# Layer kernel on one core: attention's output turned on VectorE in 32x32 blocks, the first norm's rows turned by transposing transfers, the weights' low halves made on VectorE

## What is computed

```python
mod = (_silu(c) @ wmod).reshape(8, 6, 1, 256)
sa, ca, ga, sb, cb, gb = (mod[:, i] for i in range(6))
h = layernorm(x) * (1 + ca) + sa
x = x + ga * attention(h, w_qkv, w_o)     # 16 heads of 16, causal, softmax
h = layernorm(x) * (1 + cb) + sb
x = x + gb * (shared_ffn(h) + routed_experts(h))   # 8 experts, 2 per token
```

## Time and profile before

| | us |
|---|---|
| median of the runs | 1907.32 |
| the profiled execution | 1906.43 |
| its span | 1904.7 |
| PE busy | 1759.5 (92%) |
| VectorE (DVE) busy | 1506.3 (79%) |
| ScalarE (ACT) busy | 1126.2 (59%) |
| GpSimd (POOL) busy | 955.2 (50%) |
| mean granted TensorE clock | 0.971 |

### The profile page before, as it was taken

How to read it: one execution, slowest core, us unless ns; L and a number is a source line. 1 busy time by engine, 2 the same in 40 slices (tenths; PEclk the granted TensorE clock), 3 DMA queues, 4 the chain that set the end, 5 groups by cost and what they waited for, 6 DMA issues and landing times. The chain is left out here.

```text
span 1904.7 us, 46834 instructions
## 1 busy us (share of the span) xinstructions
PE 1759.5 (92%) x17886; PEld 1014.6 (53%) x17886; DVE 1506.3 (79%) x2717; ACT 1126.2 (59%) x1486; POOL 955.2 (50%) x1015
## 2 busy tenths in 40 slices
PE   5677899999999999999999999999999999989987
PEld 2233435455554454445454545454545788778764
DVE  7886788887988787788878888988896486755777
ACT  2687867676767576767666766776676333222211
POOL 2444555365436553654454554545555267534423
PEclk8788999999999999999999999999999999999989
DMA  4243331223122312231122122221312777766997
GB/s 144 74 150 84 119 70 44 68 58 97 24 74 55 96 32 66 56 96 41 58 58 85 44 60 54 83 63 47 85 52 83 167 159 165 176 142 145 276 315 260
DMA packets 248840, 191.58 MB, mean 101 GB/s; under 512 B 181344, under 2 KB 216936, under 8 KB 246832
## 3 DMA queue, kind: packets, MB, share of 16 engines
q1 hardware_dynamic: 235472, 152.26, 32.1%
q0 software_dynamic: 12960, 36.06, 5.5%
q10 hardware_dynamic: 192, 0.26, 0.1%
HBM read 65.23 MB, written 62.19 MB: 67 GB/s over the span
## 5 line engine op out<-in xcount | busy, mean ns | idle before, releaser
L1176 ACT ACTIVATE arena<-pair 128x1024 f32<-128x1024 f32 (+1 forms) x640 | 575.5, 942 | 195.3 <-PE pair L1898 192.4
L1370 DVE TENSOR_REDUCE max_part<-pair 128x2 f32<-128x1024 f32 (+2 forms) x448 | 535.0, 1219 | 95.6 <-PE pair L1874 91.7
L1935 PE MATMUL pair<-feat_parts,ffn_sb 128*128 128x512 f16 x1536 | 379.0, 383 | 9.9 <-DMA feat_parts<-rows 5.4
L1920 PE MATMUL pair<-arena,v_sb 128*32 128x256 f32 (+1 forms) x5120 | 325.1, 367 | 2.0 <-ACT arena L1176 1.0
L950 POOL TENSOR_SCALAR_AFFINE_SELECT arena<-arena 128x512 f32<-128x512 f32 x256 | 169.5, 670 | 290.7 <-ACT arena L1176 290.4
L1874 PE MATMUL pair<-arena 48*128 48x128 f16 (+3 forms) x2304 | 209.9, 280 | 40.7 <-DMA arena<-parts 13.5
L1898 PE MATMUL pair<-arena 50*128 50x256 f16 (+1 forms) x2560 | 210.4, 264 | 22.6 <-DVE max_part L1370 7.9
L1935 PEld LDWEIGHTS pair<-feat_parts,ffn_sb 128*128 128x128 f16 x1536 | 132.7, 98 | 179.5 <-issue 38.6
L1959 PE MATMUL pair<-parts,arena 128*128 128x256 f16 x1704 | 209.6, 282 | 18.5 <-DMA parts<-lists 10.0
L1036 POOL DMA_INDIRECT slots<-arena,feat x142 | 145.0, 1021 | 145.9 <-DVE arena L1599 116.0
L1042 POOL TENSOR_TENSOR hidden<-silu_h,hidden 128x512 f16<-128x512 f32 x128 | 151.4, 1187 | 121.0 <-ACT hidden L1211 120.0
...
## 6 DMA issues: line engine op xcount, KB each, us to landing
...
```

Source lines behind the costliest of these rows:

```text
L1176: sc.activation(to[:, :, lo:QC], of[:, :, lo:QC], ACT.Exp, scale=SCALE / QK_SCALE ** 2).then_inc(exp_done, 1)
L1370: return vec.tensor_reduce(to, of, AX.X, ALU.max)
L1920: last = mm(to[32 * j:32 * j + 32, lo:QC], v_sb[:, kt, h:h + 32], probs[:, u % RING, at + lo:at + QC], start=(kt == 0), stop=(kt == 2 * c ...
L1935: last = mm(to[:, 0:512], w_up[s][W_PART[i]][:, f, m * RH + h * P:m * RH + (h + 1) * P], feat_parts[:, A_PART[i], f, c * 512:(c + 1) * 512 ...
```

## The change

Attention's output no longer goes through PE. VectorE reads the accumulator bank itself and transposes it in 32x32 blocks into `o_raw` (`turn_raw`), which leaves each head's columns in a block of its own; reciprocals and products then read `o_raw` in SBUF and write `o_tok` in a blocked order, seen as `o_blocks`. For each quarter of a batch one more VectorE transpose of 128x512, in place (`turn_o`), gives features on partitions; ScalarE casts it straight into `o_feat` and GpSimd subtracts there. The transposing transfers of the output go. The rows of w_o are loaded in the order that this leaves the features in, by eight small loads.

The first norm of batches 1 to 7 is modulated in rows: `norm1` is 16 instructions, with shift and scale rows that are loaded per batch (`load_gates1`) from a small DRAM tensor. ScalarE casts half the tiles at a time (`head_rows`), GpSimd subtracts (`head_rest`), and SyncE turns them with eight transposing transfers (`turn_head`). Batch 0 keeps the old way. The weights' units are scaled and cast in one ScalarE pass, and VectorE makes the low half in one instruction. `ORDER_OF` and `BANK_OF` are written anew; `turn_out` and, but for the start, `turn` are gone from them, and `head` is new. The diff, cut to its core:

```diff
...
-        scores:37 scores:38 scores:39 normalise:4 normalise:5 values:35 values:36 values:37 scores:40
...
+        scores:21 normalise:1 max:2:5 max:2:6 select_max:2:5 share:3 normalise:2 qk:3 scores:22 max:2:7 values:18 values:19 values:20 raw:3 values:21 max:2:8
...
+            def load_gates1(hb):
+                if hb == 1:
+                    sp.wait_ge(mod1_stored, 16)
+                    sp.wait_ge(wo_ready, 3)
+                else:
+                    sp.wait_ge(v_moved, hb)
+                sp.dma_start(gates1[:, :, :].rearrange("p m n -> p (m n)"), mod1_dram[bass.ds(hb, 1), :].to_broadcast([P, 2 * D])).then_inc(gates1_in, 16)
+
+            def turn_head(hb, h):
+                sp.wait_ge(head_low, at_half(hb - 1, h))
+                if h == 0:
+                    sp.wait_ge(qk_full, at_group(hb - 1, NG - 1))
+                    sp.wait_ge(v_full, at_half(hb - 1, 1))
+                for t in range(4 * h, 4 * h + 4):
+                    sp.dma_start_transpose(feat1_parts[:, :, :, t * P:(t + 1) * P].rearrange("p a f n -> p (a f) n"),
+                                           feat_rows[:, t, :]).then_inc(feat1_in[h], 16)
...
-            def turn_o(f, c):
-                sp.wait_ge(o_low, f * O_SPLIT + c + 1)
-                sp.wait_ge(feat1_low, at_half(min(f + 1, B - 1), 1))
-                if past(f):
-                    sp.wait_ge(op_full, at_half(f - 1, 1))
-                for t in range(2 * c, 2 * c + 2):
-                    sp.dma_start_transpose(o_feat[:, :, :, t * P:(t + 1) * P].rearrange("p a f n -> p (a f) n"),
-                                           rows16[:, t, 0:2 * D]).then_inc(o_in[c // 2], 16)
...
-            for dst, src in ((wv_in, w_v), (wo_in, w_o), (rw_in, router_w), (bias_sb[:, :], bias)):
+            for dst, src in ((wv_in, w_v), (rw_in, router_w), (bias_sb[:, :], bias)):
...
+            for j in range(GH):
+                for a in range(2):
+                    to, of = 32 * j + HD * a, GH * HD * a + HD * j
+                    sp.dma_start(wo_in[to:to + HD, :, :], w_o[of:of + HD, :, :]).then_inc(wo_landed, 16)
+
+            sp.wait_ge(mod1_made, 1)
+            sp.dma_start(mod1_dram, mod_sb).then_inc(mod1_stored, 16)
...
-            def head_low(hb, v, i):
-                pool.wait_ge(feat1_whole, at_half(hb, i))
-                pool.wait_ge(feat1_ready, at_half(hb, i))
-                gp.tensor_tensor(feat1_parts[:, 1, i, :], whole1(v, i), feat1_parts[:, 0, i, :], ALU.subtract).then_inc(feat1_low, 1)
+            def head_rest(hb, h):
+
+                pool.wait_ge(head_high, at_half(hb - 1, h))
+                t = slice(4 * h, 4 * h + 4)
+                gp.tensor_tensor(feat_rows[:, t, D:2 * D], rows[:, t, :], feat_rows[:, t, 0:D], ALU.subtract).then_inc(head_low, 1)
...
-                t = slice(2 * c, 2 * c + 2)
-                gp.tensor_tensor(rows16[:, t, D:2 * D], o_tok[:, t, :], rows16[:, t, 0:D], ALU.subtract).then_inc(o_low, 1)
+                of = o_blocks[:, c, :].rearrange("p (f n) -> p f n", f=NF)
+                t = slice(c * QC, (c + 1) * QC)
+                gp.tensor_tensor(o_feat[:, 1, :, t], of, o_feat[:, 0, :, t], ALU.subtract).then_inc(o_low, 1)
...
-            def share_low(n):
-                pool.wait_ge(w_high, n + 1)
-                to = ffn_sb[:, n, :, :] if n < NS else expert_sb[n % 2]
-                gp.tensor_tensor(to[:, 1, :], stage[n % 2], to[:, 0, :], ALU.subtract).then_inc(w_low, 1)
...
+            def head_rows(hb, v, h):
+                if h == 0:
+                    if v == "first":
+                        act.wait_ge(mods_full, 1)
+                    else:
+                        act.wait_ge(op_full, at_half(hb - 2, 1))
+                        for c in range(2):
+                            act.wait_ge(feat1_in[c], (hb - 1) * TURNED)
+                act.wait_ge(norm1_ready, hb * NT + 4 * h + 4)
+                t = slice(4 * h, 4 * h + 4)
+                sc.activation(feat_rows[:, t, 0:D], rows[:, t, :], ACT.Copy).then_inc(head_high, 1)
...
-            def raw_copy(b, n):
-                act.wait_ge(values_done, at_unit(b, end_of(n)))
-                if past(at_step(b, n - 2)):
-
-                    act.wait_ge(out_turned, at_step(b, n - 2))
-                sc.activation(o_raw[:, n % 2, :], gathered(b, n), ACT.Copy).then_inc(raw_ready, 1)
...
-                sc.activation(stage[n % 2], stage[n % 2], ACT.Copy, scale=W_SCALE).then_inc(w_scaled, 1)
-                act.wait_ge(w_scaled, n + 1)
-                sc.activation(to, stage[n % 2], ACT.Copy).then_inc(w_high, 1)
+                sc.activation(to, stage[n % 2], ACT.Copy, scale=W_SCALE).then_inc(w_high, 1)
...
-                        act.wait_ge(o_ready, at_step(f, STEPS - NQ + c))
-                        act.wait_ge(head_turned, at_half(min(b, B - 1), 1))
+                        act.wait_ge(o_turned, f * O_SPLIT + c + 1)
+                        for h in range(2):
+                            act.wait_ge(feat1_in[h], min(f + 1, B - 1) * TURNED)
                         if past(f):
-                            act.wait_ge(listed_done, at_half(f - 1, 1) * LISTED)
-                        sc.activation(rows16[:, 2 * c:2 * c + 2, 0:D], o_tok[:, 2 * c:2 * c + 2, :], ACT.Copy).then_inc(o_high, 1)
+                            act.wait_ge(op_full, at_half(f - 1, 1))
+                        sc.activation(o_feat[:, 0, :, c * QC:(c + 1) * QC], o_blocks[:, c, :].rearrange("p (f n) -> p f n", f=NF), ACT.Copy).then_inc(o_high, 1)
...
                 dve.wait_ge(inv1_ready, hb + 1)
+                if hb:
+                    dve.wait_ge(gates1_in, hb * 16)
+                    for t in range(NT):
+                        vec.scalar_tensor_tensor(rows[:, t, :], rows[:, t, :], mean_var[:, t, 0:1], gates1[:, 1, :],
+                                                 ALU.subtract, ALU.mult).then_inc(dve_step, 1)
+                        count[0] += 1
+                    dve.wait_ge(dve_step, base + count[0])
+                    for t in range(NT):
+                        vec.scalar_tensor_tensor(rows[:, t, :], rows[:, t, :], rstd[:, 1, t:t + 1], gates1[:, 0, :],
+                                                 ALU.mult, ALU.add).then_inc(norm1_ready, 1)
+                    return
...
+            def turn_raw(b, n):
+                if past(at_step(b, n - 2)):
+                    dve.wait_ge(o_ready, at_step(b, n - 2))
+                dve.wait_ge(values_done, at_unit(b, end_of(n)))
+                vec.transpose(o_raw[:, n % 2, :], gathered(b, n)).then_inc(raw_ready, 1)
+
+            def normalise(b, n, base):
                 g, c = n % STEPS // NQ, n % NQ
-                dve.wait_ge(out_turned, at_step(b, n))
-                o = buffer_of(v, ("to", n))[:, 0:QC].rearrange("p (k n) -> p k n", k=2 * GH)
+                dve.wait_ge(raw_ready, at_step(b, n))
+                o = o_raw[:, n % 2, :].rearrange("p (q r) -> p q r", r=32)
                 chain(vec.reciprocal(l_inv[:, n % 2, :], o[:, :, HD]), base)
-                to = o_tok[:, 2 * c:2 * c + 2, g * GH * HD:(g + 1) * GH * HD].rearrange("p t (j d) -> p t j d", j=GH)
-                vec.tensor_tensor(to, o[:, :, 0:HD].rearrange("p (t j) d -> p t j d", j=GH),
-                                  l_inv[:, n % 2, :].rearrange("p (t j) -> p t j", j=GH).unsqueeze(3).to_broadcast([P, 2, GH, HD]),
-                                  ALU.mult).then_inc(o_ready, 1)
+                to = o_blocks[:, c, QC * (g // 2):QC * (g // 2 + 1)].rearrange("p (q a d) -> p q a d", a=2, d=HD)[:, :, g % 2, :]
+                vec.tensor_tensor(to, o[:, :, 0:HD], l_inv[:, n % 2, :].unsqueeze(2).to_broadcast([P, 2 * GH, HD]), ALU.mult).then_inc(o_ready, 1)
+
+            def turn_o(f, c):
+                dve.wait_ge(o_ready, at_step(f, STEPS - NQ + c))
+                vec.transpose(o_blocks[:, c, :], o_blocks[:, c, :]).then_inc(o_turned, 1)
...
+                    elif kind == "share":
+                        n = at[0]
+                        dve.wait_ge(w_high, n + 1)
+                        to = ffn_sb[:, n, :, :] if n < NS else expert_sb[n % 2]
+                        vec.scalar_tensor_tensor(to[:, 1, :], stage[n % 2], W_SCALE, to[:, 0, :], ALU.mult, ALU.subtract).then_inc(w_low, 1)
...
+            def features_in(hb, halves):
+                if hb == 0:
+                    pe.wait_ge(feat1_low, at_half(0, 1))
+                else:
+                    for h in halves:
+                        pe.wait_ge(feat1_in[h], hb * TURNED)
+
             def qk(b, v, g):
                 to = take(b, v, ("qk", g))
-                pe.wait_ge(feat1_low, at_half(b if g >= EARLY else b + 1, 1))
+                features_in(b if g >= EARLY else b + 1, range(2))
...
-            def turn_out(b, v, n):
-                pe.wait_ge(raw_ready, at_step(b, n))
-                to = take(b, v, ("to", n))
-                for t in range(QC // P):
```

(4 more changed lines are left out.)

435 lines of the change are left out of this document (212 added, 223 removed).

## The result

| | before | after |
|---|---|---|
| median of 4 runs each | 1907.74 us (1906.16 to 1912.40) | 1926.58 us (1921.27 to 1931.95) |
| ratio, 95% interval | | 1.0105 (1.0074 to 1.0136) |
| profiled execution, its span | 1906.4, 1904.7 us | 1921.27, 1919.7 us |
| PE, VectorE busy | 1759.5, 1506.3 us | 1738.2, 1620.5 us |
| ScalarE, GpSimd busy | 1126.2, 955.2 us | 1057.0, 924.1 us |

The change makes the kernel 1.0% slower. The forecast was 1878 us; the result lies just above the top of its range.

A forecast was written before the change was run, and what follows sets the result against it. The prediction took PE to set the batches' pace. Loop -27, first batch 0 and end -2 made -29 us from 1906.4, so 1877.4, and 1878 us as the median; range 1848 to 1925 us.

The forecast's parts named there:

- PE, what is removed: Each loop batch loses 32 output and 16 norm row transposes on PE, taken as 7 us a batch.
- VectorE, what is added: New transposes and a longer first norm add 13.6 us a batch (12.0 to 20.0), 153.7 becoming 167.3 us.
- reciprocal and multiply stay: nothing: In attention's output on VectorE, these keep their number and width, so they add nothing.
- Rival 4: VectorE's transposes cost their upper bound, 173.7 us of work and 186.8 us a batch; 1924 us, chance 0.09.
- The loop: From 304 to 1450 us, VectorE 93% busy gives 179.9 us a batch, 4.4 less; -27 us over 6.2 batches.
- Rival 3: VectorE becomes the loop's bound with its waits kept, PE waiting for accumulator banks; 1946 us, slower, chance 0.14.
- The 3.0 us that it had against itself: Evidence against rival 3: PE's waits for VectorE at its largest line summed to only 3.0 us a batch.
- The first batch: From 62 to 304 us, VectorE rises to 225 us and the bound moves from ScalarE; 0 us, within 8.
- The head's transfers hidden: Work between the first norm and query matmuls hides the longer chain with eight transfers, 11.6 us of queue.
- the end -2: Output features skip eight transfers before the last output projections, saving 2 us.
- The list of what would show it wrong: Signs against the forecast: transposes of 0.6 us or more, waits beyond 10 us a batch, first batch past 312 us.

The follow-up runs named there:

- e13: The changed kernel with each step's product right behind, reading PSUM, without the 128 VectorE transposes, multiplying by 1e-6 instead of the reciprocal; 1.0007 of the kernel before.
- e3: The whole change written into the order of work of the kernel before; 1.0678 of the kernel before.

## Why the prediction was wrong

- **PE, what is removed** (7 us a batch): not given back. PE's busy time fell by 2.9 us, so the 7 itself looks too high, and its idle time rose by 5.9. e13 shows no gain from it with most of VectorE's burden gone.
- **VectorE, what is added** (+13.6 us, 167.3 a batch): right as a total, 166.6. The two kinds of transpose measured 0.438 and 0.687 us (0.42 and 0.69 forecast). One line was wrong, "reciprocal and multiply stay: nothing": the product grew by 55.1 - 37.3 = 17.8 us in all, 2.2 a batch, and 11 of L1336's 56 instructions took over 0.7 us (mean 0.593, median 0.474), so some of them look held as well. Rival 4 is out. The 311 ns for a 128x128 transpose that the Trainium skill's VectorE: DVE Perf Modes, section The three transpose paths, gives for bf16 would be 622 for 256 columns, an estimate from that page. 438 were measured here, on float32.
- **The loop** (167.3 / 0.93 = 179.9, 4.4 us less a batch): this step failed. The 93% was taken from 50 us in which VectorE had reached 91%, and stretched over a whole batch. Measured was 166.6 / 186.8 = 89%. The order that was run did not hold even the 91% of those 50 us over a batch, and PE's waits for VectorE rose from 1.9 to 26.3 us. For the five batches -22 had been forecast and +14.9 came. That is 37 of the 44 us between the forecast for one execution (1877.4) and the profiled one (1921.3). The next largest piece lies in the 1.2 batches behind them, priced in the same way: -5 forecast, some +8 measured (the last product of attention's output starts 281.2 us behind the last batch's first norm, 273.0 before).
- **Rival 3** (0.14) is what happened. Its deciding point was 17.0 us of VectorE idle a batch; 20.2 remained, and the batch came out 3.0 us longer. It had the place half right: PE waits for VectorE, but 13.4 us at the buffers of the maxima, not at the accumulator (the matmuls of the values wait 1.6 us for maxima and 1.0 for the transposes in the whole span). The 3.0 us that it had against itself are waits of the weight loads, which run beside PE; PE's own waits for VectorE were 1.9 us in five batches. Its price was too high (22 us idle, 1946 us).
- **The first batch** (0, VectorE to 225 us, the bound moving): right in time. It ended at 305.4 us, 1.0 later, with VectorE at 73.68 + 147.38 = 221.1 of 243.4 us and ScalarE at 164.8 (165 forecast). PE's granted clock was 0.86 from 140.5 us on, where the kernel before had 0.96 from 149.4.
- **The head's transfers hidden, the end -2**: the first is right in the changed kernel (PE waits 0.6 us for them in five batches). The end was priced too low. Everything behind the last batch's first norm is 0.9 us shorter although attention's last product comes 8.2 us later in it, so the rest of it gained some 9 us. Why is open. e3 shows what the transfers cost without cover: 12.0 us of PE's time at four places.
- The list of what would show it wrong had "PE's waits for VectorE's reductions grow beyond 10 us a batch"; all its waits for VectorE grew by 4.9 (26.3 us in five batches, 1.9 before), and the forecast was wrong all the same. The test asked too much: PE's idle time rose by 5.9 us, which is nearly all of the 7 that were to be won.
